# The prologue of an attention and expert block: when Wq's, Wkv's and Wo's low parts are made, and what the first queries wait for

## The reference

```python
xn = layer_norm(layernorm(x), ln_g, ln_b); cn = layer_norm(ctx, cln_g, cln_b)
q = (xn @ Wq) * 64 ** -0.5                      # 16 heads of 64
k, v = split(cn @ Wkv)                          # one head of 64, shared
out = softmax(q @ k.T) @ v @ Wo                 # attention over the 128 context tokens
h, gate = split(xn @ Wff1)                      # 1024 each
x = x + tanh(g_xattn) * (out + silu(gate) * h @ Wff2)
# then on layernorm(x): 8 experts of width 256, the best 2 for each token, and a shared one
x = x + tanh(g_ffn) * (experts(x) + shared(x))
```

## Time and profile before

| | us |
|---|---|
| median of 3 runs (538.79 to 539.93) | 539.51 |
| the profiled execution | 539.47 |
| its span in the trace | 537.8 |
| PE busy | 503.8 (94%) |
| DVE busy | 409.4 (76%) |
| ACT busy | 327.1 (61%) |
| Pool busy | 288.5 (54%) |
| mean granted clock of TensorE | 0.982 |

### The profile page before, as it was taken

How to read it: one execution, slowest core, us unless ns; L and a number is a source line. 1 busy time by engine, 2 the same in 40 slices (tenths; PEclk the granted TensorE clock), 3 DMA queues, 4 the chain that set the end, 5 groups by cost and what they waited for, 6 DMA issues and landing times.

```text
span 537.8 us, 13926 instructions
## 1 busy us (share of the span) xinstructions
PE 503.8 (94%) x4026; PEld 485.3 (90%) x4026; DVE 409.4 (76%) x1254; ACT 327.1 (61%) x1092; POOL 288.5 (54%) x330
## 2 busy tenths in 40 slices
PE   8789999999999999999999999999998889999980
PEld 7779999999999999999999999999997779889870
DVE  7687878688787878878887878787778887777760
ACT  3576656766675666566567565756665636666650
POOL 3487626454552655264355536444676315488763
PEclk9889999999999999999999999999999999999995
DMA  5551300021003000300301030023598965688853
GB/s 176 189 188 50 99 2 32 31 78 52 31 20 117 31 30 14 114 32 20 117 22 33 7 122 26 10 79 100 198 320 331 380 229 107 112 128 137 134 69 39
DMA packets 40212, 53.85 MB, mean 100 GB/s; under 512 B 4597, under 2 KB 34218, under 8 KB 39146
## 3 DMA queue, kind: packets, MB, share of 16 engines
q1 hardware_dynamic: 31856, 41.48, 23.2%
q0 software_dynamic: 8000, 11.86, 11.9%
q10 hardware_dynamic: 314, 0.01, 0.0%
HBM read 28.15 MB, written 25.21 MB: 99 GB/s over the span
## 4 chain that ended last, share of the span: by engine, by line
PE 66%; DVE 15%; issue 6%; ACT 5%; POOL 3%; DMA 2%; DVEq 1%; SPq 0%; POOLq 0%; ACTq 0%
PE bank L1523 14%; PE bank L1525 12%; PE bank L1524 12%; PE bank L1604 5%; PE bank L1709 4%; PE bank L1616 4%; PE bank L1699 4%; PE bank L1620 3%; PE bank L1607 2%; PE bank L1714 2%; PE bank L1538 2%; DVE norm_probs L988 2%; ACT norm_probs L803 1%; DMA spare<-in_L_xattn_Wq 1%; POOL weights L587 1%
## 5 line engine op out<-in xcount | busy, mean ns | idle before, releaser
L616 POOL TENSOR_TENSOR norm_probs<-norm_probs,rden 128x512 f32<-128x512 f32 x64 | 66.5, 1040 | 100.0 <-DVE rden L1168 99.2
L1523 PE MATMUL bank<-acts,weights 128*128 128x256 f32 x384 | 110.1, 287 | 3.4 <-POOL weights L587 3.4
L1524 PE MATMUL bank<-acts,weights 128*128 128x256 f32 x384 | 108.7, 283 | 0.0
L1525 PE MATMUL bank<-acts,weights 128*128 128x256 f32 x384 | 108.4, 282 | 0.0
L803 ACT ACTIVATE norm_probs<-bank,nmax 128x128 f32<-128x128 f32 x256 | 90.4, 367 | 23.4 <-DVE nmax L1124 23.4
L621 POOL TENSOR_TENSOR acts<-uf,acts 128x256 fp32r<-128x256 f32 x64 | 47.5, 741 | 68.7 <-ACT acts L791 68.7
L1523 PEld LDWEIGHTS bank<-acts,weights 128*128 128x128 f32 x384 | 73.3, 191 | 4.1 <-issue 3.0
L727 POOL DMA_INDIRECT out_x<-norm_probs,th x39 | 60.8, 1558 | 29.3 <-ACT norm_probs L916 16.7
L1525 PEld LDWEIGHTS bank<-acts,weights 128*128 128x128 f32 x384 | 73.2, 191 | 0.0
L1524 PEld LDWEIGHTS bank<-acts,weights 128*128 128x128 f32 x384 | 73.1, 190 | 0.0
L791 ACT ACTIVATE acts<-uf 128x256 fp32r<-128x256 f32 x64 | 26.8, 418 | 61.8 <-DVE uf L1193 61.7
(11 more groups left out here) (250 smaller groups left out, 1567.1 us busy)
## 6 DMA issues: line engine op xcount, KB each, us to landing
parked<-stage SPq DMA_DIRECT2D x12, 512.0 KB, 3.5
weights<-parked SPq DMA_DIRECT2D x6, 1024.0 KB
slot_rows<-tf SPq DMA_DIRECT2D x8, 680.0 KB, 6.5
spare<-slot_rows SPq DMA_DIRECT2D x39, 136.0 KB
ct<-in_ctx SPq DMA_DIRECT2D x8, 256.0 KB, 2.7
xs<-in_x SPq DMA_DIRECT2D x8, 256.0 KB, 4.5
stage<-in_L_ffn_up_w SPq DMA_DIRECT2D x8, 256.0 KB, 2.8
stage<-in_L_ffn_down_w SPq DMA_DIRECT2D x8, 256.0 KB, 3.1
```

The source lines that it names most:

```text
L616: pool.tensor_tensor(pr[:, s % 2], pr[:, s % 2], rden[:, s % 2, :].unsqueeze(2).broadcast_to((P, 4, P)), ALU.mult).then_inc(probs_ready, 1)
L1523: pe.matmul(ps, wts[1], mov[0], start=first, stop=False, skip_group_check=True)
L1524: pe.matmul(ps, wts[0], mov[0], start=False, stop=False, skip_group_check=True)
L1525: return pe.matmul(ps, wts[0], mov[1], start=False, stop=last, skip_group_check=True)
```

## The change

Four things are moved, and nothing of the arithmetic is changed or left out.

- `LO_PARTS` lets a chunk's semaphore count parts: two for chunks 1 and 2, four for chunk 4. `split(eng, n)` without a part waits for all of them. QP0 and QP1 wait for part 1 of chunks 1 and 2, that is for the first 512 columns; QP2 (in iteration 0) waits for the rest. The projection through Wff2 waits for as many pieces of chunk 4 as the step has reached.
- On DVE wq0's low part is made in two halves: columns 0 to 511 where the whole stood, columns 512 to 1023 behind cnT's low part. Wkv's cast and subtraction (`key_weights`) move behind xnT's low part, the gate weights' split behind the values' low part, and the first Wff1 quarter (`early_lo(3)`) ahead of both query subtractions.
- On Pool `split_lo(5)`, Wo's first half, moves from before iteration 0 into its step 0, behind the probabilities' multiplication and u's low part and ahead of `split_lo(6)`.
- SP's wait before the load of chunk 5 is on both halves of wq0's low part, since the wait is for the whole chunk; its wait before chunk 4 is on Wkv's subtraction, as before.

Its core:

```diff
+LO_PARTS = {1: 2, 2: 2, 4: 4}
...
-            eng.wait_ge(chunk_split_done[n] if n < NCA else ring_ready, 1 if n < NCA else n - NCA + 1)
+            if n >= NCA:
+                eng.wait_ge(ring_ready, n - NCA + 1)
+            else:
+                eng.wait_ge(chunk_split_done[n], LO_PARTS.get(n, 1) if part is None else part)
...
-                done.then_inc(chunk_split_done[n], 1)
+                    if (i + 1) % (4 // LO_PARTS.get(n, 1)) == 0:
+                        done.then_inc(chunk_split_done[n], 1)
...
+                    if first and s == 0:
+                        split_lo(5)
                     if first:
                         for n in CHUNK_SLOT.get(s, []):
                             split_lo(n)
...
             split_lo(4)
-            split_lo(5)
             iteration(0, first=True)
...
-            def early_lo(n):
+            def early_lo(n, part=0):
                 src, hi, lo = chunk_split(n)
                 dve.wait_ge(chunk_hi_done, n)
+                if n == 1:
+                    src, hi, lo = [t[:, 512 * part:512 * part + 512] for t in (src, hi, lo)]
...
             transposed("TXx", None, False, False, 0)
-            early_lo(1)
+            early_lo(1, 0)
             first_lo(xnT, 1, xnT_ready)
+            key_weights()
             transposed("TXc", None, False, False, 0)
+            dve.wait_ge(down_rows_in, 32)
+            dve.tensor_tensor(down_rows, down_rows, shared_rows, ALU.add).then_inc(down_sums_done, 1)
+            first_lo(cnT, 2, cnT_ready)
+            early_lo(1, 1)
+            early_lo(3)
+            queries_lo(0, None, False, False, 0)
+            queries_lo(1, None, False, False, 0)
+            keys_lo(None, False, False, 0)
+            values_lo(None, False, False, 0)
             gate_cols = cols[:, :, 5:NROW]
             dve.tensor_copy(gw_t[:, 0], gate_cols).then_inc(gw_done, 1)
...
+                if first and pair == 2:
+                    split(pe, 1)
+                    split(pe, 2)
...
-                        chunk([4, 8][(s - 1) // 4])
+                        chunk([4, 8][(s - 1) // 4], s if s < 5 else None)
...
-            split(pe, 1)
-            split(pe, 2)
+            split(pe, 1, 1)
+            split(pe, 2, 1)
```

More of the change, by code:

```diff
@@ L443, in landed, with split @@
             eng.wait_ge(stage_full[buffer(n)[1]], stage_value(n))
-        def split(eng, n):
-            eng.wait_ge(chunk_split_done[n] if n < NCA else ring_ready, 1 if n < NCA else n - NCA + 1)
+        def split(eng, n, part=None):
+            if n >= NCA:
+                eng.wait_ge(ring_ready, n - NCA + 1)
+            else:
+                eng.wait_ge(chunk_split_done[n], LO_PARTS.get(n, 1) if part is None else part)
         def turned_values(b):
@@ L1041, in queries_lo, with key_weights @@
                                   q[0][:, 2 * pair:2 * pair + 2, :].bitcast(F32), ALU.subtract).then_inc(mix_freed, 1)
-            def early_lo(n):
+            def early_lo(n, part=0):
                 src, hi, lo = chunk_split(n)
                 dve.wait_ge(chunk_hi_done, n)
+                if n == 1:
+                    src, hi, lo = [t[:, 512 * part:512 * part + 512] for t in (src, hi, lo)]
                 dve.tensor_tensor(lo, src, hi.bitcast(F32), ALU.subtract).then_inc(chunk_split_done[n], 1)
+            def key_weights():
+                landed(dve, 0)
+                kv = stage[:, 0, 0:KT * P].rearrange("p (k n) -> p k n", k=KT)
+                dve.tensor_copy(wkv[0][:, :, :], kv).then_inc(kv_hi_done, 1)
+                dve.wait_ge(kv_hi_done, 1)
+                dve.tensor_tensor(wkv[1][:, :, :], kv, wkv[0][:, :, :].bitcast(F32), ALU.subtract
+                                  ).then_inc(chunk_split_done[0], 1)
             for t in (*kz, *vv):
@@ L1063, in _ @@
             dve.wait_ge(cols_done, 1)
[L1065 to L1070, removed]
             def first_lo(dst, count, ready):
@@ L1083, in _ @@
             dve.tensor_tensor(gw_t[:, 1], gate_cols, gw_t[:, 0].bitcast(F32), ALU.subtract).then_inc(gw_done, 1)
[L1084 to L1091, removed]
             def attended_lo(u):
@@ L1624, in iteration, with chunk @@
             def iteration(g, first=False, last=False):
-                def chunk(n):
+                def chunk(n, part=None):
                     if first:
-                        split(pe, n)
+                        split(pe, n, part)
                 def scores(s):
```

## The result

The changed kernel took **542.7 us** in the median (15 runs, 541.45 to 544.52), the kernel before 539.93 in the runs beside it (15 runs, 538.79 to 542.41): a ratio of 1.0051, 95% interval 1.0038 to 1.0064. It is slower by 2.7 us. The forecast was 540.5 with a range to 542.4. The profiled execution took 541.45 us around a span of 539.7, with a mean granted clock of 0.982, as before. It is the fastest of the 15, so the 1.25 us from there to the median stand in no trace.

What follows compares the result with a forecast made beforehand. TensorE was taken as the bound, so iteration 0's delay reaches the end: -0.25 (FF2 earlier) + 1.5 (low clock) - 0.2 (slack) = +1.05 us on 539.47, giving 540.5 us, range 538.5 to 542.4.

Steps and rivals of the forecast that it cites:

- exponentials of step 3: ACT's exponentials for s = 3 in iteration 0, expected at 43.6 us instead of 42.60.
- Loads: SP's later loads behind wq0: chunk 5 lands at 21.5 us, hidden with 0.8 us of cover; later queued loads move too.
- First queries: TensorE's first query matmuls in the prologue: start at 14.6 us instead of 16.32, bounds 14.3 and 15.2.
- cnT's low part: DVE's subtraction for the scaled context in the prologue: ends at 17.3 us, where it ended before.
- FF0: TensorE's work after the values, waiting for the second query subtraction: starts at 20.25 us instead of 22.36.
- first maxima: First largest scores of iteration 0: due at 22.7 us, 2.1 us earlier than before (1.6 to 2.7).
- Pool's order: Pool's chunks 5 and 6 take 5.6 us, to 33.9; the third hidden tile (FF2) gains only 0.25 us.
- The clock: Low clock from FF2 after TensorE's 4.5 us wait: +1.5 us (0.7 to 2.2), less 0.2 of slack.
- Rival 1: Clock does not fall at FF2, or falls where it does not matter: 539.1 us, no change; chance 0.12.
- rival 3: Won time reaches the end, later steps not hanging on FF2 or its slow start absorbed: 537.4 us; chance 0.14.
- rival 4: DVE's chain 0.6 us faster (2.7 won), clock costs only 0.7: 539.1 us, no change; chance 0.06.
- Rival 2: TensorE's pauses between keys, values and FF0 bring the low clock at 20.5 us already: +2.55, 542.0 us; chance 0.18.

Runs made afterwards that it cites:

- e1: Changed kernel with Pool splitting chunk 5 before iteration 0 again: 539.39 us, ratio 1.0008 to the kernel before.
- e2: Kernel before with only chunk 5's split moved into step 0 on Pool: 543.88 us, ratio 1.0076.
- e4: Changed kernel with 30 idle identity transposes on TensorE between the scores of step 2 and FF2: 540.58 us, ratio 1.0024.
- e5: Changed kernel with Pool taking chunk 6 ahead of chunk 5 in step 0: 539.50 us, ratio 1.0000.
- e6: Changed kernel with both halves of wq0's low part made at the early place again: 541.83 us, ratio 1.0050.
- e8: e7 with Pool's part of chunk 6 moved into step 0, between the probabilities and u's low part: 537.92 us, ratio 0.9971.
- e3: Changed kernel with SP loading chunk 6 ahead of chunk 5: 541.63 us, ratio 1.0050.
- e7: Changed kernel with chunks 5 and 6 exchanged throughout: 6 loaded, rounded and split before iteration 0, 5 in step 0: 537.30 us, ratio 0.9957.
- e10: e7 with 15 identity transposes on TensorE ahead of the transposed probabilities of step 0: 535.85 us, ratio 0.9940.

## Why the prediction was wrong

**The mechanism stood, one term was missing.** Chunk 5 in front of chunk 6 on Pool sets FF2, the early probabilities help nobody, the clock falls behind the pause, and iteration 0 carries its delay to the end: e1, e2, e4 and e5 each show their part. The exponentials of step 3 came at 45.14 instead of 43.6. They are 2.54 us later than before, not 1.05. The term that was missing is the landing of chunk 6, under **Loads** below.

**First queries** at 13.82, below the bound of 14.3. xnT's low part ended at 13.67, as forecast (13.7), although it took 1.10 us beside Pool instead of 0.69. It was Pool that was earlier: its first two pieces, which I had ending at 13.1 and 14.5, ran as

```profile
11.26 1.88 POOL L591 TENSOR_TENSOR weights<-spare,weights 128x256 fp32r<-128x256 f32 x2 [6.99 <-ACT weights L874]
```

and were done by 13.14, so TensorE waited for xnT alone. No low clock came here, as forecast; the kernels fill the time ahead of the first queries with 20 transposes of the identity of their own, which the forecast left out. **cnT's low part** ended at 17.60 (forecast 17.3), **FF0** started at 20.59 (20.25), the **first maxima** at 23.09 (22.7). So the gain was 1.75 us and not 2.1. Most of it is cnT: the Wkv cast took 0.82 us where I counted 0.3, beside Pool. That is 0.35 us of the miss.

**Loads** is the step that failed: the landing of chunk 6, which the sum puts at nothing. I put a cover of 0.8 us on chunk 5's landing and wrote that everything behind it moves with it, and then never worked out when chunk 6 lands. Its issue moved from 16.24 to 19.72, behind three transfers as before, and its landing to 26.3: issues of that kind took 5.4 us in the changed kernel's trace between 14 and 28 us, 3.7 in that of the kernel before between 10 and 30. DMA's share was 1.01 to 1.07 in the microseconds from 23 to 26. ACT waited 1.03 us, in front of the rounding of u. An estimate from these numbers: with 3.7 us from the issue of its second transfer at 20.3 the chunk would have landed near 24.0, ahead of ACT's need at 25.3, so the late issue alone would have been hidden, and the longer flight made it a wait. With 0.35 and 0.1 in small pieces this makes rounded u 1.5 us later than my 27.55 (28.63 + 0.42 = 29.05). That puts FF2 at +1.28 where I had -0.25, a difference of 1.53. e6 shows it from the other side: issued 0.72 us earlier, the wait is 0.25, and FF2 stands 0.79 us nearer to the first maxima.

**Pool's order.** Chunks 5 and 6 took 5.54 us (5.6 forecast), and FF2 began 0.14 behind the last piece. Had u been rounded when I thought, 1.5 us earlier, FF2 would by this subtraction have begun at 33.99, against the 33.95 of the forecast.

**The clock.** Forecast +1.5 and 0.2 of slack back, measured from FF2 to the exponentials of step 3 9.65 us against 8.39: +1.26. The size was right. The long pause was 3.41 us, not 4.5, because the matmuls before it ran late and at the low clock.

**The rivals.** Rival 1 (539.1 on record; its own terms give 539.47 - 0.45 = 539.0) fell with the low clock at FF2, rival 3 (537.4) with FF2's wait, rival 4 (539.1) with first maxima that won less, not more. Rival 2's time, 542.0, lay nearest, but its mechanism didn't happen in the profiled execution of the changed kernel: its stretch from 20 to 28 us had the full clock. It did happen in e8, by the same prologue (below). Whether it came in other runs of the changed kernel is open: the five that took longest of the 15 (543.33 to 544.52 us) had a mean granted clock of 0.976 to 0.979, the ten others 0.981 to 0.988, so those five held more low clock, in a place that no trace shows. The two errors, 0.35 and 1.15 us, both point to later, and the upper end of the range, which ended 0.3 us short, held nothing for the second. Of the 2.2 us between forecast and median, 0.4 are not the change's: the kernel before had 539.51 us when the sum was made and 539.93 in the runs beside the changed one. By the ratio, 1.0051 of 539.51 is 542.3, just inside the range; the increase itself, 2.7 us where 1.05 was forecast, is wrong by either count.

## What to carry to other kernels

When a piece of an in-order engine's work moves, ask of each piece behind it when it is wanted: here the engine had 3.5 us of idle time before the wanted chunk, and the unwanted one went behind it. Exchanging two calls took back the loss, and with the wanted chunk in that idle time, and the earlier prologue, the kernel was 0.4% faster than the one before. Where an edit delays one issue on a queue, work out the landing of every transfer behind it up to its user, with the landing time of a full queue; loading in another order than the engine that takes the data (e3) only moves the wait.

## What the runs showed of the hardware

**How long the low clock lasts varies.** Behind one pause it was 3.4 us in the kernel before and about as long in the changed one (a mean of 0.53 over 3.58 us), but in e5 it held from 30 to 36 us, over FF2 and its pause of 0.77 us alike:

```profile
30.00:32.00 2.00, 2.00 (x11) 0.50 0.00 0
32.00:34.00 2.00, 1.23 (x6) 0.50 0.00 0
34.00:36.00 2.00, 2.00 (x11) 0.50 0.00 0
```

**The same prologue gets it or not.** The pauses ahead of the keys (0.80 to 0.84 us) and of the values (1.29 to 1.30 us) left the clock at 1.00 in the changed kernel and in e7, but in e8, with the same code and the same pauses up to there, the microsecond at 22 had

```profile
22.00:23.00 1.00, 1.00 (x6) 0.50 1.00 343
```

where e7 had

```profile
22.00:23.00 1.00, 1.00 (x11) 1.00 0.74 231
```

The first maxima of e8 are 0.94 us later than e7's, though its first queries and keys started 0.3 us earlier. This is rival 2, in a profiled execution of another kernel.

**Transposes of the identity can hold the clock, and need not.** In e10 the clock stood at 1.00 over the 1.8 us that they filled, and behind them; in e4 it rose to 1.00 while they filled a wait of 3.4 us. But in e1 the kernel's own 20 transposes ahead of the first queries ran at the low level, behind a pause of 1.68 us, and took 4.01 us instead of the 2.35 in the changed kernel. TensorE's stretch in e1:

```profile
12.00:14.00 2.00, 2.00 (x11) 0.50 0.00 0
```

The Trainium skill, TensorE: Matmul & The Clock Gate, section "What's actually happening", says that throttling is the default and activity releases it. e4 and e10 agree, with 1.00 behind the transposes in both; e1 adds that the full clock did not come at once, with TensorE busy for all of the 2 us shown.

**VectorE and GpSimd side by side: 0.7 us of luck.** In e7 VectorE's first two subtractions, beside GpSimd's pieces, took 1.15 and 1.22 us; in e10, with the same code up to there, 0.68 and 1.03, so that its first maxima came 0.68 us earlier. A gain of that size read from one trace of this prologue needs its timed runs beside it.
